# Mamba-2 layer on one core: transposes and scan moved ahead of the x block, DVE's convolution taps moved behind the scan's sum

## The reference, cut to what matters

```python
xn = _layernorm(x)
proj = xn @ in_proj_w.T                       # gate 8192, xBC 8192+2048, dt 128 channels
gate, xBC, dt = split(proj)
xBC = silu(conv4(xBC) + conv_b)               # causal convolution, 4 taps per channel
xs, B, C = split(xBC)                         # 128 heads of 64; B, C: 8 groups of 128
dt = clip(softplus(dt + dt_bias), .001, 100); cs = cumsum(dt * A)    # chunks of 128 tokens
Y = tril(exp(cs_l - cs_s)) * (C @ B.T) @ (xs * dt) + state part + xs * D
yg = Y * silu(gate); yg = yg * rsqrt(mean(yg**2 over a group of 1024) + eps) * norm_w
s = yg @ out_proj_w.T
out = x + s * silu(mixture_of_experts(xn))    # 16 experts, top 2
```

## Time and profile before

| | |
|---|---|
| median of 3 runs | 1733.6 us (1731.6 to 1734.77) |
| the profiled execution: its time / its span | 1733.94 / 1731.8 us |
| PEld, DVE, ACT, POOL busy | 75%, 86%, 59%, 53% |
| mean granted TensorE clock | 0.991 |
| the chain that ended last | PE 73%, DVE 15%, issue 7% |

### The profile page before, as it was taken

How to read it: one execution, slowest core, us unless ns; L and a number is a source line. 1 busy time by engine, 2 the same in 40 slices (tenths; PEclk the granted TensorE clock), 3 DMA queues, 4 the chain that set the end, 5 groups by cost and what they waited for, 6 DMA issues and landing times.

```text
span 1731.8 us, 31320 instructions
## 1 busy us (share of the span) xinstructions
PE 1670.0 (96%) x9236; PEld 1307.0 (75%) x9236; DVE 1492.6 (86%) x1729; ACT 1028.1 (59%) x1601; POOL 924.9 (53%) x593
## 2 busy tenths in 40 slices
PE   7699989999999999999999999999999999999996
PEld 5477867777777777777777777777777777777775
DVE  6533698898999899998999899989999899989996
ACT  4233476666666667666666666566666666665751
POOL 3442265555565555565565556555655555555652
PEclk9799999999999999999999999999999999999999
DMA  3332222212221122122222222222221222122204
GB/s 120 111 96 69 76 76 71 65 52 66 76 66 52 64 78 71 58 58 64 79 64 57 59 72 69 60 59 71 77 59 46 76 72 62 61 60 74 70 21 146
DMA packets 73458, 121.39 MB, mean 70 GB/s; under 512 B 12366, under 2 KB 17870, under 8 KB 73252
## 3 DMA queue, kind: packets, MB, share of 16 engines
q1 hardware_dynamic: 72676, 117.92, 22.7%
q10 hardware_dynamic: 576, 1.05, 0.2%
HBM read 112.64 MB, written 6.29 MB: 69 GB/s over the span
## 4 chain that ended last, share of the span: by engine, by line
PE 73%; DVE 15%; issue 7%; ACT 2%; POOL 1%; DMA 1%; DVEq 0%; SPq 0%; ACTq 0%; POOLq 0%
PE pj L455 13%; PE pj L457 12%; PE pj L456 12%; PE sc L625 6%; PE ob L455 6%; PE ob L456 5%; PE ob L457 5%; DVE conv L1229 3%; PE seg L604 3%; PE tb L614 3%; PE sc L629 3%; DVE wo_lo L1293 2%; DVE decay L1257 2%; DVE xc L1243 1%; DVE yT_lo L1285 1%
## 5 line engine op out<-in xcount | busy, mean ns | idle before, releaser
L966 POOL TENSOR_TENSOR w_lo<-stg,w_hi 128x512 fp32r<-128x512 f32 x316 | 514.3, 1628 | 430.4 <-ACT w_hi L832 335.8
L455 PE MATMUL pj<-xT_hi,w_hi 128*128 128x512 f32 x1208 | 480.8, 398 | 7.6 <-DVE conv L1229 5.1
L456 PE MATMUL pj<-xT_lo,w_hi 128*128 128x512 f32 x1208 | 472.1, 391 | 0.0
L457 PE MATMUL pj<-xT_hi,w_lo 128*128 128x512 f32 x1208 | 472.1, 391 | 0.0
L1229 DVE SCALAR_TENSOR_TENSOR conv<-pj,par,conv 128x510 f32<-128x510 f32 (+2 forms) x480 | 357.2, 744 | 60.1 <-ACT conv L840 47.8
L996 POOL TENSOR_TENSOR xc<-xc,thg 128x512 f32<-128x512 f32 x128 | 202.5, 1582 | 259.8 <-DVE xc L1280 259.8
L1257 DVE TENSOR_TENSOR decay<-decay,gm 128x1536 f32<-128x1536 f32 x128 | 282.7, 2209 | 0.0
L455 PEld LDWEIGHTS pj<-xT_hi,w_hi 128*128 128x128 f32 x1208 | 227.3, 188 | 66.6 <-DVE conv L1229 8.1
L457 PEld LDWEIGHTS pj<-xT_hi,w_lo 128*128 128x128 f32 x1208 | 227.3, 188 | 49.1
L456 PEld LDWEIGHTS pj<-xT_lo,w_hi 128*128 128x128 f32 x1208 | 227.5, 188 | 45.1
L455 PE MATMUL ob<-wo_hi,yT_hi 128*128 128x512 f32 x540 | 223.3, 414 | 7.4 <-DVE part L1306 4.9
(11 more groups left out here) (169 smaller groups left out, 2270.6 us busy)
## 6 DMA issues: line engine op xcount, KB each, us to landing
stg<-wstream SPq DMA_DIRECT2D x387, 256.0 KB, 2.7
rowt<-cs_scr SPq DMA_DIRECT2D x384, 4.0 KB
colt<-cs_scr SPq DMA_DIRECT2D x384, 4.0 KB
acc<-hid SPq DMA_DIRECT2D x8, 256.0 KB, 4.7
decay<-gate_scr SPq DMA_DIRECT2D x8, 256.0 KB, 4.1
xc<-hid SPq DMA_DIRECT2D x8, 256.0 KB, 5.4
out<-acc SPq DMA_DIRECT2D x8, 256.0 KB, 2.0
gate_scr<-part SPq DMA_DIRECT2D x4, 256.0 KB, 2.0
```

The source lines that it names most:

```text
L455: nc.tensor.matmul(dst, hi_w, hi_x, start=first, stop=False)
L456: nc.tensor.matmul(dst, hi_w, lo_x, start=False, stop=False)
L457: return nc.tensor.matmul(dst, lo_w, hi_x, start=False, stop=last)
L966: nc.gpsimd.tensor_tensor(w_dest(n, 1), stg[:, s % RING, :], f32(w_dest(n, 0)), ALU.subtract).then_inc(S["wl"], 1)
```

## The change

In the step of PE the calls of `x_turn` and `scan` go in front of the first x block (and of `bc_products`); in the step of DVE `x_times_dt` and `add_scan` go in front of `taps` of the first x block (and of `mask_products`). ACT, POOL and SP are as before.

```diff
@@ PE, step
                 if s == 1 and with_out:
                     square_sums(g, half)
+                if has_pair(g, half, s + 1):
+                    x_turn(*pair(g, half, s + 1))
+                if has_pair(g, half, s):
+                    scan(g, half, s)
                 if mine:
                     channel_block(g, half, mine[0])
                 if s == 5 and not is_last(g, half):
                     bc_products(*following(g, half))
-                if has_pair(g, half, s + 1):
-                    x_turn(*pair(g, half, s + 1))
-                if has_pair(g, half, s):
-                    scan(g, half, s)
                 if s != 5 and has_pair(g, half, s + 2):
                     exponents(*pair(g, half, s + 2))
@@ DVE, step
                 if has_pair(g, half, s + 1):
                     block_weights(*pair(g, half, s + 1))
+                if has_pair(g, half, s + 1):
+                    x_times_dt(*pair(g, half, s + 1))
+                if has_pair(g, half, s):
+                    add_scan(g, half, s)
                 if mine:
                     taps(g, half, mine[0])
                 if s == 5 and not is_last(g, half):
                     mask_products(*following(g, half))
-                if has_pair(g, half, s + 1):
-                    x_times_dt(*pair(g, half, s + 1))
-                if has_pair(g, half, s):
-                    add_scan(g, half, s)
                 for m in mine[1:]:
                     taps(g, half, m)
```

## The result

The changed kernel takes 1810.39 us (median of 4 runs, 1808.73 to 1812.15); the kernel before took 1733.44 us beside it (1731.6 to 1734.77). The ratio is 1.0443, interval 1.0429 to 1.0457: slower by 77 us. The profiled execution has a span of 1807.9 us, 76.1 more than before, and a mean granted clock of 0.982 instead of 0.991.

What follows compares the result with a forecast made beforehand. PE, busy 96% of the span, was taken as the bound. Shape changes 24.5, mean-square waits 5.8 + 26.5, mask-product waits 11.2 + 15.4 and clock 6 made 89.4 us: 1733.6 + 89.4 = 1823 us, 5.2% slower, range 1780 to 1850.

Steps and rivals of the forecast that it cites:

- changes of shape: PE's steps with scan and x block, outside step 5: one more change of matmul shape, 102 x 0.24 = 24.5 us.
- `msq`, both halves: Step 1 of PE: transposes wait for the mean square the x block covered; 5.8 us in half 0, 26.5 in half 1.
- `gm`, both halves: Step 5: exponents of pair 7 wait for later mask products; 11.2 us in half 1, 15.4 in half 0.
- clock: Lower granted clock behind the seven waits of about 4 us, charged at half: 7 x 0.5 x 1.7 = 6 us.
- PE's other waits: Scan's waits for `u`, `w` and `xdt`, and SP's loads: priced at 0.
- ahead of the first square sums: First half, steps without an output block, where DVE is the slower engine: 0, plus or minus 4 us.
- `msq` in half 0: Step 1: transposes stand still 0.84 us for the chain from PE's gate block, 7 times, 5.8 us.
- `msq` in half 1: Step 1, DVE behind: 3.5 us of new wait, 7 times, and about 2 us in group 0: 26.5 us.
- faster: Rival, chance 0.05: earlier add_scan shrinks DVE's lag in half 0, waits of 5.2 us and some first-half time go: 1724.
- The bubble: Steps 4 and 6, between two x blocks: DVE idle 1.3 to 2 us ahead of the second taps.
- the clock falls at every long wait: Rival, chance 0.10: all 22 new waits of 1.6 to 4 us lower the clock, 37 us instead of 6: 1854.
- Half the waits arrive: Rival, chance 0.22: only half of the forecast waits come, 24.5 + 58.9/2 = 54 us: 1788.

Runs made afterwards that it cites:

- exponents moved too: Against the changed kernel, the exponents stand directly behind the scan, in front of the x block, outside step 5: 1808.97 us, ratio 1.0437.

## Why the prediction was right in direction and 13 us too high

| term | forecast | measured | by |
|---|---|---|---|
| changes of shape | 102 x 0.24 = 24.5 | 102 x 0.225 = 23 | step distances; exponents moved too |
| `msq`, both halves | 5.8 + 26.5 = 32.3 | 6.7 | steps 1 of before and after |
| `gm`, both halves | 11.2 + 15.4 = 26.6 | 34.9 | sums of waits |
| clock | 6 | 19 | 12 falls at 1.6, from the lengths of steps |
| PE's other waits | 0 | -4.3 | sums of waits |
| ahead of the first square sums | 0 | -2.8 | their starts |
| sum | 89.4 | 76.5 (span: 76.1) | |

That the sum is only 13 us off is in part luck: `msq` is 26 us too high, `gm` and the clock together are 21 us too low, and 7 us that went elsewhere were not forecast.

**Changes of shape: right.** The 0.24 us read from step 5 held for every other step at 0.22 to 0.24, and went when the exponents followed the scan. The reading that 0.24 is peculiar to step 5, a bound of 0, is excluded.

**`msq` in half 0: right.** 0.70 us against 0.84, the chain from PE's own gate block.

**`msq` in half 1: the step that failed.** It is the sentence "DVE is busy 37.6 of the 38 us before this, so whatever the change adds to DVE's stretch arrives here in full". The additions were counted, and what the change takes away was not: the prediction had `add_scan` as one that "serves POOL, which is no bound", and against its own rival of a shrinking lag it held that "nothing was taken out of DVE's stretch". What was taken out is duration. Beside POOL's product and the `w_lo` behind it `x_silu` and `wo_lo` took 1.76 and 1.78 us; after, 0.69 and 0.75. With 2 us less in each step of half 0 the lag of 2.5 us (3.98 - 1.44) cannot build up. The row that would have said so was in reach: 259.8 us of POOL idle for `add_scan`, ahead of an instruction beside which the next two of DVE take twice their time. The Trainium skill, SBUF — State Buffer, Who interferes with whom, says that a VectorE instruction with two SBUF inputs contends with a GpSimd instruction that reads SBUF, and one with at most one such input, outside the 2-port modes, does not. The traces agree: L1243 and L1293 have two and move between 0.7 and 1.8 us; `gate_silu` (L1272), with one of its two inputs in PSUM, starts beside a running POOL instruction 79 times before and 51 times after and never takes more than 0.69 us.

The rival "faster" had the right mechanism: DVE's lag shrinks, and it is gone. Its condition was not met: it asked for a mean square within 0.6 us of the square sums, and in half 1 this starts 1.43 us behind them (912.78 to 914.21), as in half 0 before, because the chain from PE's gate block stays. And it drops all other terms, which the lag does not touch.

**`gm`: right in place, too small.** Forecast were waits of 1.6 and, with the 0.4 of today, 2.6 us; measured 2.6 and 2.5 to 3.0. The order was priced nearly right (step 5 of DVE in the old order: 1.25 us back of 1.34), and so was the later start of the second taps (1.1 us against PE in half 1, forecast 1.0). In half 1 the missing 1.0 us is overlap that has moved: the second `x_silu` of B and C stands between the second taps and `gm`, and it has grown by 1.1 us. Before and after:

```profile
739.33 0.68 DVE L1243 SCALAR_TENSOR_TENSOR bc<-thx,conv 128x512 f32<-128x512 f32 x1
```

```profile
762.16 1.78 DVE L1243 SCALAR_TENSOR_TENSOR bc<-thx,conv 128x512 f32<-128x512 f32 x1
```

POOL's sum of squares (L1002) starts at 761.77 after, ahead of this instruction; before it starts at 739.80, behind it. `y_lo` and `add_output` of the same stretch are unchanged (1.42 and 1.44, 1.78 and 1.76 us). That attribution rests on durations and was not tried by itself.

**The bubble: right size, two causes named and one of them wrong.** The idle time ahead of the second taps is 1.8 us, inside the 1.3 to 2 forecast. The prediction gives both "nothing stands there" and ACT's queue; the run with steps 4 and 6 in the old order leaves the queue alone as the cause, and its working by that queue (1.0 us later) was right.

**The clock: right price, a third of the size.** I charged 7 waits of about 4 us on `msq` at half of 1.7 us. None of that length came; the 14 waits on `gm`, of 2.5 to 3.0 us, were not charged at all, and 12 of them lowered the clock, for 1.6 us each. The rival "the clock falls at every long wait" (22 x 1.7) was thus nearer on the waits that came; what keeps the time far below its 1854 is that 8 of its 22, those on `msq`, stayed at 0.7 us, and no fall followed them.

**Half the waits arrive** (1788) had the right reason, "DVE's instructions take 1.4 to 1.8 us where POOL runs beside them", and applied it evenly instead of to the one wait that is made of DVE's lag. The result lies between it and the forecast: 1810 of 1823, within the range of 1780 to 1850.

## What to carry to other kernels

When an instruction moves, ask not only what waits for it but what it releases on an engine that is "no bound", and beside whose instructions that will then run: here 87 us of POOL's and 53 us of DVE's busy time went without one instruction fewer. A wait at the end of a lag is priced by the whole stretch in which the lag builds up; a wait on a fixed chain by the chain. And a change in two parts is worth splitting: the half that moved PE cost all that was lost and more, while a part of the half that moved DVE, kept out of the steps where DVE is asked for something urgent, makes the kernel 0.6% faster.

## What the runs showed of the hardware

**The clock behind a wait.** Over the traces of these 14 kernels, between 300 and 1690 us, in a stream of PE that is otherwise full, I counted the waits behind which at least three full-width products started 0.41 to 0.44 us apart within 7 us:

| length of the wait | waits | followed by the lower level | products at it, where it came |
|---|---|---|---|
| 0.6 to 1.0 us | 106 | 0 | |
| 1.0 to 2.0 us | 65 | 11 | 3 to 8 |
| 2.0 to 2.55 us | 17 | 8 | 3 to 8 |
| 2.55 us and over | 58 | 52 | 5 to 11 |

The counts are a floor: five more falls, behind waits on `msq` of 1.3 to 2.6 us, fell on narrow products and show only two such rows each. The lengths of steps price a fall at about 1.6 us with 5 to 7 full-width products and 3.0 us with 11. So the price of a wait isn't proportional to it: one of 2.6 us nearly always costs 1.6 us more through the clock, one of 0.7 us nothing. It isn't the place alone: 57 of the 58 longest waits stand on `gm`, and so do 24 of the 106 shortest. The Trainium skill, TensorE: Matmul & The Clock Gate, What's actually happening, has the lower clock as the default which activity lifts; the rows agree in so far as a wait of over 1.0 us stood ahead of every fall counted, and show in addition that none of the 106 waits of 0.6 to 1.0 us brought one.

**Costs taken away elsewhere changed this count.** With the waits on `gm` unchanged at 38 us, 68 products ran at the lower level in the changed kernel and 110 without the wait on `msq`. 8.4 of the 14.5 us won went that way. I have no cause for it.

**A change of matmul shape** between 512-wide full-depth products, the 64-column scan and the 6-row exponents costs 0.22 us each time, and reordering removes it.
